# GpSimd makes six of the 32 low parts of the expert weights in a two-layer attention and mixture-of-experts kernel

## The reference

```python
x = x + attention0(layernorm(x), ctx, ctx)             # 16 heads, with biases
x = x + moe(layernorm(x))                              # 8 experts, top 2
x = x + attention1(ctx, ctx, layernorm(x), mask)       # shared 16x16 head matrices
x = x + spiking_ffn(layernorm(x))                      # 5 threshold steps

def moe(x):                                            # x: 128 sequences x 128 rows x 256
    top_vals, top_idx = top_k(x @ Wg + bg, 2)
    out = 0
    for i in range(2):
        e = top_idx[..., i].reshape(-1)[:batch]        # one expert per sequence
        h = gelu(x @ W1[e] + b1[e])                    # W1: 8 x 256 x 1024
        out += softmax(top_vals)[..., i] * (h @ W2[e] + b2[e])   # W2: 8 x 1024 x 256
    return out
```

## Time and profile before

| what | value |
|---|---|
| median of 3 runs | 3892.73 us (3887.35 to 3898.45) |
| the profiled execution, its time | 3895.72 us |
| the profiled execution, its span | 3893.9 us |
| TensorE, share of the span | 95% |
| VectorE, ScalarE, GpSimd, share of the span | 79%, 57%, 57% |
| mean granted TensorE clock | 0.979 |

### The profile page before, as it was taken

The page is one execution under the profiler, slowest core; times in us unless marked ns, Lnnn a source line. Parts: engine busy times, 40 slices in busy tenths (PEclk is TensorE's granted clock), DMA queues, the critical chain, the costliest instruction groups (busy, mean ns, idle before and its releaser), DMA issues. The chain is left out here.

```text
span 3893.9 us, 134428 instructions
## 1 busy us (share of the span) xinstructions
PE 3698.4 (95%) x47408; PEld 2873.8 (74%) x47408; DVE 3089.8 (79%) x5266; ACT 2206.1 (57%) x4529; POOL 2201.1 (57%) x3316
## 2 busy tenths in 40 slices
PE   5999999994899999999999996999999989999999
PEld 4777777772777777777777774566666668888888
DVE  4888888886777777777777775798889867777777
ACT  3777777775444444444444442677667764555554
POOL 5666666663354533333333334466656667887777
PEclk9999999997999999999999997899999999999999
DMA  4677777775322322222222223699999963332332
GB/s 124 189 210 203 213 207 220 215 203 170 91 78 80 81 68 71 64 74 62 74 64 72 66 69 87 160 215 210 212 210 215 204 148 77 81 76 74 78 78 69
DMA packets 834241, 502.59 MB, mean 129 GB/s; under 512 B 262037, under 2 KB 824408, under 8 KB 833480
## 3 DMA queue, kind: packets, MB, share of 16 engines
q1 hardware_dynamic: 832680, 493.49, 50.5%
q0 software_dynamic: 928, 0.49, 0.1%
HBM read 251.27 MB, written 214.96 MB: 120 GB/s over the span
## 5 line engine op out<-in xcount | busy, mean ns | idle before, releaser
L1506 ACT ACTIVATE all_region<-phase_loop_hid,phase_b1T 128x128 f32<-128x128 f32 x2048 | 584.5, 368 | 729.9 <-PE phase_loop_hid L193 700.2
L191 PE MATMUL phase_loop_hid<-phase_loop_moe_h,phase_w_hi 128*128 128x128 f16 x4096 | 728.4, 220 | 0.1
L192 PE MATMUL phase_loop_hid<-phase_loop_moe_h,phase_w_hi 128*128 128x128 f16 x4096 | 726.5, 220 | 0.0
L193 PE MATMUL phase_loop_hid<-phase_loop_moe_h,phase_w_lo 128*128 128x128 f16 x4096 | 726.5, 220 | 0.0
L1112 DVE TENSOR_REDUCE phase_loop_mx<-phase_loop_score 128x8 f32<-128x1024 f32 x512 | 625.7, 1222 | 105.1 <-PE phase_loop_score L875 97.9
L1472 PE MATMUL phase_loop_moe_y<-phase_w,all_region 128*128 x2048 | 693.9, 380 | 0.2
L1030 ACT ACTIVATE phase_loop_pt<-phase_loop_scoreT 128x1024 f32<-128x1024 f32 x448 | 458.2, 1023 | 275.0 <-PE phase_loop_scoreT L909 272.5
L1474 PE MATMUL phase_loop_moe_y<-phase_w,all_region 128*128 x2048 | 558.8, 273 | 0.0
L1524 DVE TENSOR_SCALAR all_region<-all_region 128x512 f16<-128x512 f32 x512 | 257.2, 502 | 249.4 <-PE phase_loop_moe_y L1474 193.4
L191 PEld LDWEIGHTS phase_loop_hid<-phase_loop_moe_h,phase_w_hi 128*128 x4096 | 400.2, 98 | 66.9 <-issue 0.4
L1527 DVE SCALAR_TENSOR_TENSOR all_region<-all_region 128x512 f16<-128x512 f32 x512 | 410.1, 801 | 17.6
(11 more groups left out here) (276 smaller groups left out, 9840.4 us busy)
## 6 DMA issues: line engine op xcount, KB each, us to landing
qk_scratch<-phase_loop_qk SPq DMA_DIRECT2D x192, 256.0 KB, 3.6
phase_loop_qS<-qk_scratch SPq DMA_DIRECT2D x768, 64.0 KB, 3.2
phase_loop_cin<-in_ctx SPq DMA_DIRECT2D x128, 256.0 KB, 4.6
x_scratch<-phase_loop_x SPq DMA_DIRECT2D x128, 256.0 KB, 3.1
h_scratch<-phase_loop_hr SPq DMA_DIRECT2D x128, 256.0 KB, 3.8
phase_loop_kS<-qk_scratch SPq DMA_DIRECT2D x384, 64.0 KB, 2.4
ks_scratch<-ct_scratch SPq DMA_DIRECT2D x384, 64.0 KB, 2.4
phase_loop_kS<-ks_scratch SPq DMA_DIRECT2D x128, 192.0 KB, 3.9
```

What stands on the lines that cost most here:

```text
L191: eng.matmul(out, l_hi, r_hi, start=start, stop=False)
L192: eng.matmul(out, l_hi, r_lo, start=False, stop=False)
L193: return eng.matmul(out, l_lo, r_hi, start=False, stop=stop)
L1506: i = act.activation(hf[n % NF][:, j, :], hid(u, n)[:, j * S:(j + 1) * S], ACT.Gelu, bias=w["b1"][:, bass.ds(e * HB + (4 * half + j), 1)], ...
```

## The change

The low parts of the blocks 3, 7, 11, 15, 19 and 23 are taken from VectorE and made on GpSimd. GpSimd needs two instructions for each: a multiplication of the raw block by the power of two, in place, and a subtraction of the high part. It counts them on semaphores of their own (`s_ps` between the two, `s_pl` for the finished part). The multiplication writes into the raw buffer and so waits for the high part. Where a load waits for a low part, it waits for the engine that makes it: `wait_low` replaces the wait in front of the loads. The GpSimd program is in the third part of the stage, behind the memsets and DMA issues of `prepare_shared_heads`.

```diff
@@ def prepare_experts(kk, c, w, late, io, idx_d, first_raw, s_first):
+    POOL_JOBS = (3, 7, 11, 15, 19, 23)
...
-    s_hi, s_lo, s_b, s_t, s_i = (kk.sem(f"expert_{x}") for x in ("hi", "lo", "b", "t", "i"))
+    s_hi, s_lo, s_b, s_t, s_i, s_ps, s_pl = (kk.sem(f"expert_{x}") for x in ("hi", "lo", "b", "t", "i", "ps", "pl"))
...
+    def wait_low(eng, i):
+
+        before = sum(j <= i for j in POOL_JOBS)
+        if i in POOL_JOBS:
+            eng.wait_ge(s_pl, before)
+        else:
+            eng.wait_ge(s_lo, i + 1 - before)
+
+    def gpsimd(g):
+        for n, i in enumerate(POOL_JOBS):
+            hi, lo = jobs[i]
+            g.wait_ge(s_hi, i + 1)
+            g.tensor_scalar(view(i), view(i), p2(W_X), None, ALU.mult).then_inc(s_ps, 1)
+            g.wait_ge(s_ps, n + 1)
+            g.tensor_tensor(lo, view(i), hi, ALU.subtract).then_inc(s_pl, 1)
...
-            sp.wait_ge(s_lo, i - slots + 1)
+            wait_low(sp, i - slots)
             sp.dma_start(view(i), sources[i]).then_inc(s_ld[i % slots], 16)
...
     def low(v, some):
         for i in some:
+            if i in POOL_JOBS:
+                continue
             hi, lo = jobs[i]
             v.wait_ge(s_hi, i + 1)
...
-            {"scalar": lambda act: high(act, rest), "vector": lambda v: low(v, rest)})
+            {"scalar": lambda act: high(act, rest), "vector": lambda v: low(v, rest), "gpsimd": gpsimd})
```

## The result

| | before | changed |
|---|---|---|
| first comparison: median of 14 runs each | 3891.49 us | 3894.77 us |
| ratio, 95% interval | | 1.0018 (1.0011 to 1.0024) |
| the comparison repeated: median of 27 and 12 runs | 3890.30 us | 3897.01 us |
| ratio, 95% interval | | 1.0021 (1.0012 to 1.0031) |
| the preparation stage, from a profile each | 46.70 us | 56.15 us (55.77 in the repeat) |

The kernel is slower by 0.2%: 4.3 to 9.3 us by the interval of the first comparison. The ratio is not that of the two medians, which lie only 3.3 us apart there (6.7 us in the repeat), so the size is known to a few microseconds at best. It is less than the 0.3% named as the edge of no change, though both intervals lie above 1. The stage is measured from GpSimd's first memset to SyncE's first transfer behind the meeting of the engines; it grew by 9.45 us, and by 9.07 in the repeat.

The account below looks back on a forecast made before the run. Loads, with VectorE level, were taken to bound the preparation stage. A late block 3 delays the load path 5.6 us; with turns VectorE finishes block 25 9.6 us late, so the median becomes about 3902 us, range 3894 to 3914.

Parts of the forecast that it names:

- What bounds the stage: Preparation stage: loads lead and VectorE arrives level with them at 970; freeing VectorE alone moves nothing of a hoped-for 6.8 us.
- When GpSimd can begin: Block 3 on GpSimd starts behind 27 DMA issues, at 950.13, delaying load 16 and all behind it; called the main cost.
- What one block costs: GpSimd's multiplication 2.2 us and subtraction 2.1 with 0.2 between: 4.5 us a block, bounds 3.5 and 7.9.
- The two small rows: Profile rows of GpSimd multiplications, 231 ns for 2 columns and 288 for 32: 1.9 ns a column, so 2.2 us for 1024.
- the sum: Adding up the stage: load path +5.6 us, VectorE +9.6 at block 25, stage end 992.0, median about 3902 us.
- The load path: SyncE's loads 16 to 25, issued from 955.6; the write behind them lands at 972.9 instead of 967.3: +5.6 us.
- The turns: VectorE and GpSimd hold each other up: 1.5 us per GpSimd instruction, six instructions, 9.0 us; block 25 done +9.6 us late.
- The chain behind it: From VectorE's block 25 to the end of the stage: 12.9 us, as before, with GpSimd nearly done by then.
- The total: Whole kernel: median 3892.73 + 9.5, about 3902 us, 0.24% slower, below the 0.3% that a measurement can tell.
- a sign of being wrong: Expert loop and rest behind the stage should keep their length; a change there would mean the prediction is wrong.
- The slow multiplication: First rival: GpSimd's multiplication takes 4.3 us or more, GpSimd bounds, +14 to +20; decides from about 6.5 us a block; chance 0.25.
- The third rival: Hardly any exclusion at 1024 columns, or multiplication at the cast's rate: only the load path counts, +4 to +7, 3898; chance 0.20.

Follow-up runs that it names:

- the kernel with the list aside: Kernel before, VectorE making all low parts, list through GpSimd's DMA queue, shared heads behind block 19 instead of 25: ratio 0.9999 (0.9990 to 1.0008), stage 46.83 us.
- the single block: Changed kernel with block 3 alone on GpSimd instead of six blocks: stage 52.99 us; ratio to the kernel before 1.0011 (1.0001 to 1.0021).
- the memset run: Changed kernel with GpSimd filling its six low parts with zeros by five memsets each instead of computing them: stage 53.42 us against 46.70 before.

## Why the prediction was right

* **What bounds the stage.** "Freeing VectorE alone can move nothing" holds: with three blocks taken off and no load delayed, the list and the index table stayed where they were. I had called the loads the bound and VectorE level with them; the kernel with the list aside shows how level, since with the list out of the way the stage stays at 46.8 us and ends on VectorE's own work.
* **When GpSimd can begin** held to the tenth, right behind the last DMA issue, 14.2 us into the stage; block 3 is done at 19.9 against 19.6. Load 16 went out at 943.60 before, not at 944.8, which is only the mean spacing of the nine. "This is the main cost of the change" is shown by the single block: +6.3 of +9.45.
* **What one block costs** was mis-sized. The multiplication is 2.78 us alone, not 2.2. The two small rows gave too small a slope; line 1419, 1363 ns for 256 columns, was too long by some 0.5 us if the price of 2.5 ns a column between 2 and 1024 columns holds there (an estimate from 231 ns and 2.78 us), as argued. The subtraction was exact (2.12 against 2.14). By its own words the sum should have had 4.5 + 2 x 0.57 = 5.6 us a block, not 5.4; block 3 took 5.66, and a pair in full turns takes 6.2.
* **The load path** came out later than its sum: the list is +6.9 us late, not +5.6. Block 11 was ready 1.5 us later than thought, SyncE issued load 24 right behind it (969.40), and from ScalarE's high part of block 16 to that of block 25 it is 13.7 us against 12.55 in the kernel with block 3 alone. But there, without that wait, the list is late by 6.1 us too (6.7 in the second profile). Common to all kernels with the late block is another term: SyncE gets past the write of the expert choice 1.0 to 1.8 us after the high part of block 25 begins, in place of the 0.2 of the kernel before. Why is open. Against it stands a term that was too large: from the issue of load 16 to its high part it took 3.6 us (957.30 to 960.87), not 2.1 + 1.39 + 0.9 = 4.4.
* **The turns** were over-sized where I counted them. From block 16 on the eight low parts were lengthened by 6.2 us in all (2.32, 2.05, 1.21, 2.53, 2.05, 1.21, 2.50, 2.05 less 1.21 each), against the 9.0 of the sum. Three of them met a multiplication and were held for 0.84 us each; three met a subtraction some 0.9 us after its start and were held for 1.1 to 1.3 (961.96 is one, during block 7's subtraction). Block 25 was done +7.7 us late, not +9.6. A VectorE that is never idle pays 2.76 us a pair, near the 2 x 1.5 assumed, but as 0.84 and 1.93 and not as twice the same.
* **The chain behind it** I took over as 12.9 us, "as before". It grew: from the end of block 25 to SyncE's next transfer it is 14.97 us against 13.21. GpSimd was not done: block 19's subtraction held the mask instruction (1.54 us in place of 0.20), block 23's the first of the last six low parts (2.54 in place of 1.21); in return the 0.83 us that VectorE had waited for ScalarE went. This +1.8 and the -1.9 of the point above cancel. That the stage's +9.45 comes so close to the predicted +9.6 is luck in part: its terms for the list, the turns and the chain behind were off by 1.3 to 2.8 us each.
* **The total.** +9.5 us was forecast on the median. The first comparison says 4.3 to 9.3, the second 4.7 to 12.1: inside the range (1 to 21 us above 3892.73), the first wholly within 0.3% and the second all but its upper edge. The stretch behind the stage, whose change would have been a sign of being wrong, did change its length between the two profiles, by 12.7 us in the third phase; as the other kernels, with the same code there, differ by 8 us among themselves, this sign tells nothing from one profile of each.
* **The rivals.** The slow multiplication lay between my 2.2 and its 4.3 us, and its deciding point, 6.5 us a block, was missed by 0.3. The Trainium skill ("SBUF — State Buffer", section "Who interferes with whom") has the lock held for the whole instruction. The subtraction bears that out, holding VectorE to within 0.13 us of its end, 1.93 us at most; the multiplication does not, since it held a low part for 0.84 us of its 2.78 and ran on beside it. The same section says that a VectorE instruction with two SBUF inputs contends with GpSimd's reads and not with its writes; the memset run agrees, 1.23 us at most. The third rival, no turns, is out: one pair costs VectorE 2.76 us. The Trainium skill ("GPSIMD Engine Reference", section "4.1 Engine selection") calls one-input instructions "roughly line-rate". The cast takes 1.2 ns a column here and this multiplication 2.7, so one rate does not fit both.

## What to carry to other kernels

Before moving elementwise work from a busy VectorE to GpSimd, subtract what it costs VectorE: here a pair of GpSimd instructions took 2.8 us from a VectorE that is never idle, to spare it 1.14. Look also at what stands ahead of the new work in GpSimd's queue and who is behind its result in another queue: one late buffer at the head of an in-order load queue made two thirds of the loss. And where a profile's total scatters more than the change, compare the stretch that was changed, not the span.

## What the runs showed that I had not expected

A GpSimd memset leaves VectorE's low parts, which read two tensors, alone but lengthens some of its instructions that read one. In the memset kernel four mask instructions took this long, against 0.87 us in the kernel before and 0.88 in the changed one:

```profile
981.02 1.48 DVE L1690 TENSOR_SCALAR all_mask<-prep_mask_int,prep_mask_away 128x128 bf16<-128x128 int32 x4
```

And the stage of the changed kernel is shorter than that of the one in which GpSimd's work is waited for by nobody (56.15 against 58.28 us). A stall in the loads gives GpSimd time in which VectorE has nothing to lose, but the 3.4 us of low parts that VectorE makes there in addition are more than the difference; no run separates the two.
